# A two-pass FFN kernel on one core: the second pass' weights prepared a unit at a time during the first pass

## What is computed

```python
def _L0_cond_ref(x, subjects, weights):            # x: 32 x 128 x 2048
    w = weights[subjects]
    return jnp.einsum('bct,bcd->bdt', x, w)

def _L0_ffn_ref(x, W_base, b_base, W_gate, A, B):  # 2048 -> 2048, E, R = 8, 16
    result = jnp.einsum('bnd,od->bno', x, W_base) + b_base
    logits = jnp.einsum('bnd,ed->bne', x, W_gate)
    ...                                            # softmax, best two of eight, route_w
    h = jnp.einsum('bnd,erd->bner', x, A)
    hw = h * route_w[..., None]
    delta = jnp.einsum('bner,eor->bno', hw, B)
    return result + delta * SCALING

    x = x + _L0_ffn_ref(_L0_cond_ref(x, itok_B_0_30, L0_cond_weights), ...)
```

## Time and profile before

| | us |
|---|---|
| median of three runs | 1633.84 |
| lowest and highest | 1632.02, 1634.96 |
| the profiled execution | 1634.34 |
| its span in the profile | 1632.6 |
| TensorE busy | 1536.8 |
| VectorE busy | 1300.2 |
| GpSimd busy | 631.9 |
| ScalarE busy | 596.5 |

### The profile page before, as it was taken

How to read it: one execution, slowest core, us unless ns; L and a number is a source line. 1 busy time by engine, 2 the same in 40 slices (tenths; PEclk the granted TensorE clock), 3 DMA queues, 4 the chain that set the end, 5 groups by cost and what they waited for, 6 DMA issues and landing times.

```text
span 1632.6 us, 25730 instructions
## 1 busy us (share of the span) xinstructions
PE 1536.8 (94%) x9539; PEld 837.8 (51%) x9539; DVE 1300.2 (80%) x2228; ACT 596.5 (37%) x996; POOL 631.9 (39%) x473
## 2 busy tenths in 40 slices
PE   5667999999999999999668999999999999999998
PEld 5444555555555555555464555555555555555553
DVE  6666888888888888888776888888888888888874
ACT  6654333333333333333583323333322333332231
POOL 2534455555555555555453122222212221221222
PEclk8788999999999999999889999999999999999999
DMA  5332444444444444444731344343334434333432
GB/s 198 130 117 82 128 136 136 135 135 134 128 136 136 136 127 133 132 134 125 235 104 39 98 137 136 110 122 121 102 91 136 136 113 121 122 105 88 134 107 71
DMA packets 102911, 201.87 MB, mean 124 GB/s; under 512 B 10874, under 2 KB 24186, under 8 KB 102266
## 3 DMA queue, kind: packets, MB, share of 16 engines
q1 hardware_dynamic: 102786, 200.22, 39.8%
HBM read 128.96 MB, written 71.22 MB: 123 GB/s over the span
## 4 chain that ended last, share of the span: by engine, by line
PE 89%; DVE 5%; ACT 2%; issue 2%; DMA 1%; POOL 1%; POOLq 0%; SPq 0%; DVEq 0%; ACTq 0%
PE bank_x L1121 10%; PE bank_x L1122 10%; PE bank_x L1123 10%; PE bank_y L1123 10%; PE bank_y L1122 10%; PE bank_y L1121 10%; PE bank_z L1121 3%; PE bank_z L1123 3%; PE bank_z L1122 3%; PE bank_h L1122 3%; PE bank_h L1121 3%; PE bank_h L1123 3%; PE bank_c L1121 2%; PE bank_c L1123 2%; PE bank_c L1122 2%
## 5 line engine op out<-in xcount | busy, mean ns | idle before, releaser
L475 POOL TENSOR_TENSOR x_res<-x_res,t_sums 128x512 f32<-128x512 f32 x256 | 350.7, 1372 | 895.6 <-DVE t_sums L827 735.5
L1121 PE MATMUL bank_x<-TT,s_parts 128*128 128x512 f16 x768 | 295.5, 385 | 14.8 <-POOL TT L450 7.5
L1122 PE MATMUL bank_x<-TT,s_parts 128*128 128x512 f16 x768 | 295.0, 384 | 0.0
L1123 PE MATMUL bank_x<-TT,s_parts 128*128 128x512 f16 x768 | 294.6, 384 | 0.0
L1121 PE MATMUL bank_y<-TT,s_parts 128*128 128x512 f16 x768 | 291.2, 379 | 0.0
L1122 PE MATMUL bank_y<-TT,s_parts 128*128 128x512 f16 x768 | 291.1, 379 | 0.0
L1123 PE MATMUL bank_y<-TT,s_parts 128*128 128x512 f16 x768 | 291.1, 379 | 0.0
L571 ACT ACTIVATE p_copies<-bank_x,y_inv 128x512 f32<-128x512 f32 x128 | 87.8, 686 | 492.8 <-PE bank_x L1123 398.7
L827 DVE TENSOR_TENSOR t_sums<-t_sums,inv_w 128x512 f32<-128x512 f32 x256 | 218.6, 854 | 8.8
L800 DVE TENSOR_TENSOR s_parts<-a_full,s_parts 128x512 f16<-128x512 f32 x224 | 208.1, 951 | 7.5 <-ACT s_parts L556 7.5
L456 POOL TENSOR_TENSOR x_res<-x_res,BT 128x512 f32<-128x512 f32 x128 | 197.8, 1545 | 4.8 <-DMA x_res<-in_x_dram 3.3
(11 more groups left out here) (219 smaller groups left out, 2715.6 us busy)
## 6 DMA issues: line engine op xcount, KB each, us to landing
x<-in_x_dram SPq DMA_DIRECT2D x32, 1024.0 KB, 5.7
x_res<-in_x_dram SPq DMA_DIRECT2D x128, 256.0 KB, 3.7
part_scratch<-x_res SPq DMA_DIRECT2D x128, 256.0 KB, 2.9
x_res<-part_scratch SPq DMA_DIRECT2D x128, 256.0 KB, 3.9
out_dram<-x_res SPq DMA_DIRECT2D x128, 256.0 KB, 2.8
x_parts<-in_L_ffn_W_base_dram SPq DMA_DIRECT2D x12, 512.0 KB, 5.3
a_full<-in_L_ffn_W_base_dram SPq DMA_DIRECT2D x12, 512.0 KB, 4.8
w_cond<-in_L_cond_weights_dram SPq DMA_DIRECT2D x64, 64.0 KB, 3.9
```

The costliest lines, as they stand in the source:

```text
L475: nc.gpsimd.tensor_tensor(XR[:, xr_slot(m), :], XR[:, xr_slot(m), :], TM[:, m % 2, :], ALU.add).then_inc(r_added, 1)
L1121: nc.tensor.matmul(dst, lhs[0], rhs[0], start=start, stop=False, skip_group_check=chained)
L1122: nc.tensor.matmul(dst, lhs[0], rhs[1], start=False, stop=False, skip_group_check=chained)
L1123: return nc.tensor.matmul(dst, lhs[1], rhs[0], start=False, stop=stop, skip_group_check=chained)
```

## The change

The preparation of units 8 to 15 after step 15 is gone, and so is step 16's wait for it. In its place, eight units (now called 0 to 7 of the second pass) go through the engines during the first pass. `AHEAD` says in which step's end a unit's rows are loaded, summed and scaled (steps 1, 3, 5, ..., 13, 14); the step after it carries the unit (2, 4, ..., 14, 15). The rows lie in `x_parts` after the step's last conditioning matmul, and are scaled there in place. A unit is worked in four chunks of 128 columns: TensorE turns four blocks into `bank_d` (`turn_chunk`), ScalarE copies them to `a_full` (`copy_chunk`), GpSimd forms the four sums (`add_up`), ScalarE rounds seven blocks to the upper part (`upper_chunk`), VectorE subtracts for the lower part (`lower_chunk`). Each part is a piece of 128 x 7 x 128 f16 in one of three slots (`NPIECE`) and is stored by SP to `wt_scratch` in DRAM, in runs of 256 bytes (`store_piece`). The inverse scales go to `inv_scratch`. In step 15, as each product of the first pass ends for the last time, ScalarE's queue loads that slice of `TT` (1 MB each, 14 in all, `load_weights`), and step 16's products wait slice by slice (`t_in`). To make room, `SLOTS` is 9, and h_first, hw, hwT and diag share the new tensor `late_words` with the pieces. ScalarE's `copy_p(n, 1, U2_COPY)` of the first pass moves ahead of S3's upper. A sketch of the smaller edits (names, addresses of T3, conditions of units 8 to 15) is left out below.

```diff
-SLOTS = 10
+SLOTS = 9
...
+        AHEAD = {1: 0, 3: 1, 5: 2, 7: 3, 9: 4, 11: 5, 13: 6, 14: 7}
...
+        def unit_after(n):
+            return AHEAD.get(n - 1)
...
+        def piece(g, c, part):
+            return (2 * (C4 * g + c) + part) % NPIECE
...
+        def piece_turn(g, c, part):
+            return 16 * ((2 * (C4 * g + c) + part) // NPIECE + 1)
...
+            def store_piece(g, c, part):
+                s, r = g // 4, g % 4
+                sp.wait_ge((bg_hi, bg_lo)[part], n_chunk(g, c))
+                at = piece(g, c, part)
+                sp.dma_start(wt_dram[:, s, :, part, c, r * P:(r + 1) * P].rearrange("q p n -> p q n"), pieces[:, at, :, :]
+                             ).then_inc(bg_out[at], 16)
...
             for n in range(NSTEP):
                 p, k = pair(n)
+                g = unit_after(n)
+                if g is not None:
+                    store_inv(g)
+                    store_piece(g, 0, 0)
+                    store_piece(g, 0, 1)
+                    store_piece(g, 1, 0)
+                    store_piece(g, 1, 1)
...
+                    if g is not None and j == 0:
+                        store_piece(g, 2, 0)
+                        store_piece(g, 2, 1)
+                    if g is not None and j == 1:
+                        store_piece(g, 3, 0)
+                        store_piece(g, 3, 1)
...
+                    if n in AHEAD and j == 3:
+                        sp.wait_ge(cond_done, 4 * (n + 2))
+                        load_rows_ahead(AHEAD[n])
...
                 if n == NP - 1:
+                    load_inv(1)
                     sp.wait_ge(h_out, 16 * NP)
+                    for part in range(2):
+                        sp.wait_ge(bg_out[piece(NU - 1, C4 - 1, part)], piece_turn(NU - 1, C4 - 1, part))
+                    sp.wait_ge(bg_out[piece(NU - 1, C4 - 2, 1)], piece_turn(NU - 1, C4 - 2, 1))
                     sp.dma_start(h0[:, :, :].rearrange("p b n -> p (b n)"), h_dram[0]).then_inc(h_in, 16)
...
+            def add_up(g, c):
+                chunk = full[c % 2].rearrange("p (i n) -> p i n", i=8)
+                pool.wait_ge(bg_copied, n_chunk(g, c))
+                nc.gpsimd.tensor_tensor(chunk[:, 5, :], chunk[:, 2, :], chunk[:, 0, :], ALU.subtract)
+                link(nc.gpsimd.tensor_tensor(chunk[:, 4, :], chunk[:, 0, :], chunk[:, 1, :], ALU.subtract))
+                link(nc.gpsimd.tensor_tensor(chunk[:, 6, :], chunk[:, 2, :], chunk[:, 4, :], ALU.subtract))
+                nc.gpsimd.tensor_tensor(chunk[:, 7, :], chunk[:, 6, :], chunk[:, 3, :], ALU.subtract).then_inc(bg_sum, 1)
...
+                    g = unit_after(n)
+                    if g is not None:
+                        add_up(g, 0)
+                        add_up(g, 1)
+                        add_up(g, 2)
...
+                        if g is not None and j == 0:
+                            add_up(g, 3)
...
                 act.wait_ge(cond_done, 4 * n + u + 1)
                 if n > 0 and u == 0:
                     act.wait_ge(s_lo, NPROD * n)
+                g = unit_after(n - 1)
+                if g is not None and u in (0, 2):
+                    act.wait_ge(bg_lo, n_chunk(g, 2 + u // 2))
...
+            def copy_chunk(g, c):
+                act.wait_ge(bg_tr, n_chunk(g, c))
+                if c >= 2:
+                    act.wait_ge(bg_lo, n_chunk(g, c - 2))
+                else:
+                    act.wait_ge(s_lo, NPROD * (min(n for n in AHEAD if AHEAD[n] == g) + 2))
+                nc.scalar.activation(full[c % 2][:, 0:Q], BD[:, :], ACT.Copy).then_inc(bg_copied, 1)
+            def upper_chunk(g, c):
+                act.wait_ge(bg_sum, n_chunk(g, c))
+                at = piece(g, c, 0)
+                if piece_turn(g, c, 0) > 16:
+                    act.wait_ge(bg_out[at], piece_turn(g, c, 0) - 16)
+                nc.scalar.activation(pieces[:, at, :, :], full[c % 2][:, P:8 * P].rearrange("p (q n) -> p q n", q=NPROD),
+                                     ACT.Copy).then_inc(bg_hi, 1)
...
+                act.wait_ge(prod_done, n_prod(NP - 1, s, q))
...
+                act.dma_start(TT[:, q, s, :, :, :], wt_dram[SAVED.index(q), s, :, :, :, :]).then_inc(t_in[s][q], 16)
...
+                if g is not None:
+                    copy_inv_ahead(g)
                 copy_p(n, 0, P1_COPY)
+                if fresh:
+                    load_weights(0, 0)
...
+                if g is not None:
+                    copy_chunk(g, 0)
+                    upper_chunk(g, 0)
+                    copy_chunk(g, 1)
                 copy_p(n, 0, P5_COPY)
+                if fresh:
+                    load_weights(0, 1)
+                if g is not None:
+                    upper_chunk(g, 1)
+                    copy_chunk(g, 2)
                 copy_p(n, 0, U2_COPY)
+                if fresh:
+                    load_weights(0, 2)
+                    load_weights(0, 3)
...
+                if g is not None:
+                    copy_chunk(g, 3)
+                    upper_chunk(g, 2)
                 copy_p(n, 0, P4_COPY)
+                if fresh:
+                    load_weights(0, 4)
+                if g is not None:
+                    upper_chunk(g, 3)
...
+                    copy_p(n, 1, U2_COPY)
                     s_upper(n + 1, S3)
-                    copy_p(n, 1, U2_COPY)
+                    if fresh:
+                        for q in range(5):
+                            load_weights(1, q)
...
+                if n in AHEAD:
+                    sum_rows_ahead(AHEAD[n])
                 copy_p(n, 1, P4_COPY)
...
+                if n in AHEAD:
+                    scale_rows_ahead(AHEAD[n])
...
+            def scales_ahead(g):
+                dve.wait_ge(bg_sums, g + 1)
+                power_of_two(row_pow2[:, :], row_sum[:, 0, :], row_clamped[:, :])
+                link(nc.vector.reciprocal(row_rpow2[:, :], row_pow2[:, :]))
+                if g > 0:
+                    dve.wait_ge(bg_rows_scaled, g)
+                    dve.wait_ge(bg_spread, g)
+                nc.vector.tensor_scalar(row_scale[:, :], row_rpow2[:, :], TOP_W, None, ALU.mult).then_inc(bg_scaled, 1)
...
+            def lower_chunk(g, c):
+                dve.wait_ge(bg_hi, n_chunk(g, c))
+                if n_chunk(g, c) > 1:
+                    dve.wait_ge(bg_lo, n_chunk(g, c) - 1)
+                at = piece(g, c, 1)
+                if piece_turn(g, c, 1) > 16:
+                    dve.wait_ge(bg_out[at], piece_turn(g, c, 1) - 16)
+                nc.vector.tensor_tensor(pieces[:, at, :, :], full[c % 2][:, P:8 * P].rearrange("p (q n) -> p q n", q=NPROD),
+                                        pieces[:, piece(g, c, 0), :, :], ALU.subtract).then_inc(bg_lo, 1)
...
+                if g is not None:
+                    lower_chunk(g, 0)
+                    lower_chunk(g, 1)
                 finish(n, 0, C11)
...
+                if g is not None:
+                    lower_chunk(g, 2)
                 finish(n, 0, C12)
+                if g is not None:
+                    lower_chunk(g, 3)
                 if second:
...
+                if n in AHEAD:
+                    scales_ahead(AHEAD[n])
                 finish(n, 1, C12)
...
@@ -1172,6 +1373,8 @@
                 before = 2 * n + s - 1
                 if s == 0:
                     pe.wait_ge(s_lo, n_s(n, q))
+                if n == NP:
+                    pe.wait_ge(t_in[s][q], 16)
...
+            def spread_ahead(g):
+                pe.wait_ge(bg_diag, g + 1)
+                for i in range(2):
...
+            def turn_chunk(g, c):
+                if c == 0:
+                    pe.wait_ge(bg_rows_scaled, g + 1)
+                    pe.wait_ge(bg_inv, g + 1)
+                else:
+                    pe.wait_ge(bg_copied, n_chunk(g, c - 1))
...
+                    mm = nc.tensor.transpose(BD[:, i * P:(i + 1) * P],
+                                             xp_rows[:, block_of, half * Q + c * P:half * Q + (c + 1) * P], ident[:, :])
+                mm.then_inc(bg_tr, 1)
...
+                g = unit_after(n)
                 product(n, 0, 0)
+                if g is not None:
+                    turn_chunk(g, 0)
                 make_features(n)
                 if more:
                     transpose_maxima(n + 1)
+                if g is not None:
+                    turn_chunk(g, 1)
                 for q in range(1, NPROD):
                     product(n, 0, q)
+                    if g is not None and q < 3:
+                        turn_chunk(g, q + 1)
...
+                if n in AHEAD:
+                    spread_ahead(AHEAD[n])
```

153 lines of the change are left out of this document (99 added, 54 removed).

## The result

| | before | changed |
|---|---|---|
| median, us | 1634.16 | 1657.3 |
| lowest and highest | 1632.02, 1634.96 | 1653.0, 1660.55 |
| span of the profiled execution | 1632.6 | 1658.1 |
| TensorE busy | 1536.8 | 1527.1 |

The ratio is 1.0142 with an interval of 1.0112 to 1.0172: 23 us slower, where 28 were forecast.

What follows compares the result with a forecast made beforehand. TensorE bounds each step, with one hole between the passes; 90 for eight units + 5 for steps 14 and 15 + 9.2 at the seam - 75.6 = +28.6, so 1662 us (own range 1640 to 1676; wider 1622 to 1692).

Steps and rivals of the forecast that it cites:

- Steps 14 and 15: Last two first-pass steps, both carrying a unit: late VectorE and queues shared with 7 MB of weights cost 5 us (0 to 8).
- The seam: Between the passes: h_first lands late, TensorE waits 7.2 us and a fallen clock adds 2.0; 9.2 us (6 to 14).
- The hole: TensorE's gap between the passes, 73.6 us plus 2.0 for a fallen clock: 75.6 us, all the change can win.
- Rival 4: The change does not remove the gap between the passes, since late slices keep it open; slower, chance 0.01.
- Own work and the edge: TensorE's new transposes and small matmuls, 1.9 us per unit; wait for scales at the step's edge, 1.0 us (0.8 to 1.5).
- The chain through chunk 1: Unit step: turning chunk 2 waits 2.9 us (2.3 to 3.4) for ScalarE's copy behind GpSimd's sums; then 0.95 more (0.4 to 1.6).
- The chain through the DRAM store: Chunk 3's lower parts wait until upper 2 lands in DRAM, delaying the last product: 4.4 us per unit (3.2 to 7.7).
- Rival 1, the clock: Unit steps: waits drop TensorE's clock, 2.0 us per unit, 16 in all, 1678 us; chance 0.23 together with late landings.
- So I put them at nothing: Step 15 and the seam: the fourteen 1 MB weight slices arrive in time and cost nothing.
- Rivals 2 and 3: Store lands before it is needed, 1624 us (chance 0.11); side engines hide the whole chain, 1583 us (chance 0.06).
- Its own sign of being wrong: Unit steps, forecast at 53 us: the prediction is wrong if they are under 50 us or the store lands within 3.
- the late end: Latest landing of upper 2's store, 38.4 us after the unit step's start: 5.7 more for 896 runs of 256 bytes.

Runs made afterwards that it cites:

- e12: e9 with three piece buffers in place of four; 1616.5 us, ratio to before 0.9893.
- e9: e8 plus chunk 1 copied before chunk 0's upper parts, chunk 0 and 1 sums before the first bias sum, BT and half 1 slices read after the last; 1588.4 us.
- e3: Changed kernel with ScalarE copying chunk 1 out of PSUM ahead of making the upper parts of chunk 0; 1652.8 us, ratio to before 1.0119.
- e7: Changed kernel without the 14 reads of weight slices and TensorE's waits for them, leaving out part of the computation; 1638.8 us, ratio to before 1.0034.
- e6: Changed kernel with each of TensorE's pieces of a unit put one product later; 1653.0 us, ratio to before 1.0118.
- e11: Changed kernel with earlier units, FT and h_first read at the last step's start, BT and half 1 slices after the last bias sum; 1635.2 us.
- e1: Changed kernel with h_first read in the first pass's last step, ahead of the tile loads; 1654.4 us, ratio to before 1.0138.
- e8: Changed kernel with turns one product later, four piece buffers, earlier units, chunk 3's upper parts after the first condition copy, early FT and h_first reads; 1621.2 us.

## Why the prediction was right, and where not

The sign, the places of the waits and the total hold: 104.2 us of cost were forecast and 102.0 were there. But the close total is partly luck, since errors of opposite sign stand in it. Eight units at 9.05 are 72.4 where 90 were put. Steps 14 and 15 took 10.9 more than that where 5 were put (1.28, 11.5 and 16.2 less two units of 9.05). The seam took 18.7 where 9.2 were put.

- **The hole** is gone as forecast: the interval of `transpose_maxima` around it was 117.72 us in the kernel before (755.39 to 873.11), 75.6 more than a step. Rival 4 is out.
- **Own work and the edge.** 1.9 per unit, and the step with the edge costs 1.28, of which one turn is 0.44 and the two small matmuls 0.12 (575.38 to 575.50): a wait of 0.7, where 1.0 was put (the profile marks 0.56 of it).
- **The chain through chunk 1.** 2.79 measured for 2.9, chunk 2 turned 11.96 us after the start for 11.95. Chunk 3 waits 0.65 for 0.95 where the clock stays up. Right to 0.3, though GpSimd's sums took 0.45 and not 0.37.
- **The chain through the DRAM store: the mis-sized term.** 4.4 was forecast ahead of the last product; 0.52 to 1.50 stand there. By the unit shown, in its own steps: the landing was waited for until 32.9 instead of 33.9 (1.0), the rest of the chain took 0.5 less (the product starts at 48.0, not 49.5), and TensorE itself got there at 46.9 rather than 45.1, being 1.8 late by cold matmuls and by a wait of 0.65 for a conditioning copy. 4.4 less 1.0, 0.5 and 1.8 is the 1.1 of the row. The mechanism was there (VectorE waits, and e12 has 1.7 to 3.4 us of TensorE's waits at these places when nothing covers them); its size assumed that nothing else would be late on TensorE in the meantime. A unit cost 9.05 and not 11.2: 17 us too much in eight. The sum of the range's upper end was off as well: a landing at 38.4 for 33.9 makes 4.4 into 8.9, not 7.7.
- **Rival 1, the clock,** came true in part. TensorE's waits in unit 0, then the windows behind the wait of 2.79 us in unit 4 (at 587.46, above) and in unit 0; the clock is the third number from the end:

```profile
213.80 0.66 PE L1446 MATMUL bank_d<-ident,x_parts 128*128 128x128 f32 x4 [2.79 <-ACT a_full L739]
217.69 0.66 PE L1446 MATMUL bank_d<-ident,x_parts 128*128 128x128 f32 x4 [0.65 <-ACT a_full L739]
```

```profile
588.00:593.00 5.00, 5.00 (x20) 2.25 (x19) 1.71 (x3) 1.44 (x2) 3.22 (x7) 0.68 0.54 137
214.00:219.00 5.00, 4.35 (x24) 2.17 (x23) 2.17 (x4) 1.76 (x3) 3.30 (x6) 1.00 0.51 131
```

  In unit 4 the product behind the wait takes 4.09 us for 2.59. From the turn of chunk 2 to that of chunk 3 it is 3.89 us in units 0, 5 and 6, where the clock stays up, and 4.76, 4.77, 6.03 and 4.77 in units 1 to 4. So the net price is 0.9 to 2.1 us in four of these seven units, in place of 2.0 in each. What decides between the two is not shown. In e9, whose unit steps have no wait over 1.3 us, the clock is 1.00; in e12 a wait of 2.59 us was followed by a clock of 0.76 (548 to 555), in e3 one of 2.40 was not (1.00).
- **Steps 14 and 15 and the seam: the step that failed.** "So I put them at nothing" was wrong. With the slices left out (e7) steps 14 and 15 cost 4.5 beyond two of its units (1.28, 13.3 and 6.4 less 2 x 8.24), where 5 was put, and the seam costs 10.3 (57.77 less 47.50) with a wait of 7.47, where the prediction had 9.2 and 7.2. With the slices the seam costs 18.7, and the last step 9.9 more. The seven of half 1 were not late (TensorE has no wait behind 901.54 in that step), which is what the prediction tested. They lengthened what stood beside them: tile stores from 3 to 9 us, and with SyncE in order behind these, `h_first`; in the last step VectorE waited 10.85 us for a piece's store where it was 4.2 to 4.8. Together the slices cost 18.5 us.
- **Rivals 2 and 3** fall: VectorE does wait for the store, 4.2 to 4.8 us in the units that stand alone, and the side engines do not hide the chain as the lists stand. With the lists mended they nearly do (3.2 per unit, 1.9 of it TensorE's own).
- **Its own sign of being wrong,** unit steps under 50 us, was met on the edge: 49.87 in the mean by the steps above, 50.3 from first product to first product, where 53 were forecast. It marks the mis-sized term. The other sign, a store that lands within 3 us, was not met: in the unit shown it took 4.8.

The Trainium skill (DMA: Bandwidth & Descriptors, Specifications) wants pieces of 512 bytes or more. The 64 stores of 224 KB in runs of 256 bytes landed after 2.5 to 11.4 us, 3.9 in the median, where tile stores of 256 KB in long runs took 3.1. The medians differ by 0.8 us, a small part of the 5.7 us that the late end allowed for small runs.

## What to carry to other kernels

A wait on one engine has the price that the profile shows only as long as the others stay: here the same buffer slot was worth 1.3 us or less in the first kernel and 3.6 in the mended one, and single edits (e3, e6) mostly moved a wait to the next place that needed the same late engine. So cut a late chain at all its links before judging one. And price a large background read by the small transfers beside it that someone waits for, not only by whether the read itself is in time; ask for the urgent small ones first (e11, 22 us; in e1 the read went out behind the slices, and it gave 3).

## What the runs showed of the hardware that was not expected

- A read of 136 KB on one queue landed after 14.1 us beside seven reads of 1 MB on another (e1), after 5.3 behind most of them, and after about 4.3 without them (e7).
- Issuing can be slowed beside the slices: a piece store takes SyncE 0.36 to 0.43 us in the unit step shown, and one in the last step took 3.41. (The two stores of chunk 2 took 3.90 together there, and 1.04 in e7, without the slices.) The 8.91 us of the x4 in the rows of the last steps, 5.38 in a common unit step, are four issues with SyncE's waits for the pieces between them.

```profile
845.70 3.41 SPq L381 DMA_DIRECT2D wt_scratch<-late_words  x1
```

- GpSimd's 128x128 sum takes 0.45 us alone and 1.27 at 599.57, beside VectorE's `split_x_lo`. In e8 and in e9 VectorE's `w_cond_parts` took 1.35 us instead of 0.35 beside GpSimd's addition of a 128x512 tile.
